# Local attention: the output product and its residual sum for two tiles at once, in every second slot

## The reference

```python
h = shift_token(x); q, k, v = split(h @ wqkv)      # 128 -> 3 x 512
q, k = l2norm(q) * qs, l2norm(k) * ksc
q, k = rotary_xpos(q, k)
o = local_attention(q, k, v)                       # own and previous window, masked
x = x + o @ wo                                     # 512 -> 128: product and residual sum
h = layer_norm(shift_token(x)); a, g = split(h @ w1 + b1)
x = x + (a * gelu(g)) @ w2 + b2
```

## Time and profile before

| | us |
|---|---|
| median of 3 runs | 2858.48 (2858.22 to 2858.83) |
| the profiled execution | 2855.07 |
| its span | 2853.3 |
| PE busy | 2602.7 (91%) |
| DVE busy | 2146.8 (75%) |
| ACT busy | 1946.6 (68%) |
| POOL busy | 1093.9 (38%) |

### The profile page before, as it was taken

One profiled execution on the slowest core, in us unless ns is written; L12 is line 12 of the kernel. 1 busy time (PEld: TensorE's weight loads), 2 busy tenths in 40 slices (PEclk: granted clock), 3 DMA queues, 4 the chain that ended last, 5 costly groups with the idle time before them and its releaser, 6 DMA issues. The chain is left out here.

```text
span 2853.3 us, 61208 instructions
## 1 busy us (share of the span) xinstructions
PE 2602.7 (91%) x21644; PEld 1731.2 (61%) x21644; DVE 2146.8 (75%) x3842; ACT 1946.6 (68%) x5521; POOL 1093.9 (38%) x1248
## 2 busy tenths in 40 slices
PE   6699898987989899888799999998989999999898
PEld 3476896764654444435557777776435777777643
DVE  4577565776766689667689999996448999999676
ACT  4477565776754544263289999997438999999744
POOL 0243343430005633210055555553215555555331
PEclk9799998998999999899899999999999999999999
DMA  4200120000000000130000000000000000000000
GB/s 149 78 24 25 52 76 24 24 24 7 9 17 1 1 0 1 32 61 1 28 2 2 2 2 2 2 2 21 1 9 2 2 2 2 2 2 2 2 26 34
DMA packets 83166, 53.87 MB, mean 19 GB/s; under 512 B 28848, under 2 KB 75568, under 8 KB 82864
## 3 DMA queue, kind: packets, MB, share of 16 engines
q1 hardware_dynamic: 78768, 41.56, 5.2%
q0 software_dynamic: 4096, 8.40, 1.0%
HBM read 31.59 MB, written 18.35 MB: 18 GB/s over the span
## 5 line engine op out<-in xcount | busy, mean ns | idle before, releaser
L2214 ACT ACTIVATE probs<-banks,minus_max,rnorm 128x128 f32<-128x128 f32 x1024 | 460.1, 469 | 4.3 <-DVE minus_max L2310 4.3
L2130 POOL TENSOR_TENSOR qk_cross<-qk_raw,rope_scaled 128x512 f32<-128x512 f32 x256 | 326.2, 1275 | 21.7 <-ACT qk_raw L2247 9.2
L2087 PE MATMUL banks<-weights,hf 128*128 128x512 f32 x512 | 276.8, 623 | 5.0 <-ACT kt L2243 5.0
L2140 POOL TENSOR_TENSOR qk_rot<-qk_rot,rnorm 128x512 f32<-128x512 f32 x128 | 133.5, 1043 | 284.6 <-DVE qk_rot L2343 284.1
L2214 ACT ACTIVATION_READ_ACCUMULATOR probs<-banks,minus_max,rnorm 128x1 f32 x1024 | 223.3, 218 | 0.0
L2290 DVE COPY probs_t<-banks 128x512 f32<-128x512 f32 x256 | 175.6, 686 | 46.0 <-PE banks L2053 46.0
L2053 PEld LDWEIGHTS banks<-ident,probs 128*128 128x128 f32 x1024 | 127.1, 141 | 136.7 <-issue 133.7
L731 ACT ACTIVATE probs<-banks,minus_max 128x128 f32<-128x128 f32 (+1 forms) x512 | 206.6, 437 | 4.9 <-DVE minus_max L759 4.7
L2336 DVE TENSOR_TENSOR qk_rot<-qk_raw,rope_scaled 128x512 f32<-128x512 f32 x256 | 175.0, 723 | 0.0
L2324 DVE TENSOR_REDUCE sumsq<-qk_sq 128x16 f32<-128x1024 f32 x128 | 154.7, 1208 | 23.0 <-issue 17.6
L2096 PE MATMUL banks<-ident,qk_rot 128*128 128x128 f32 x1024 | 159.1, 278 | 14.0 <-DVE qk_rot L2343 8.7
(11 more groups left out here) (357 smaller groups left out, 6903.7 us busy)
## 6 DMA issues: line engine op xcount, KB each, us to landing
sorted_x<-zero_rows SPq DMA_DIRECT2D x10, 512.0 KB, 6.0
rows_in<-sorted_x SPq DMA_DIRECT2D x18, 256.0 KB, 3.1
sorted_y<-rows_out SPq DMA_DIRECT2D x18, 256.0 KB, 2.4
x_res<-in_x SPq DMA_DIRECT2D x8, 512.0 KB, 6.6
out_x<-x_res SPq DMA_DIRECT2D x16, 256.0 KB, 2.0
w1b<-in_L_ffn_w SPq DMA_DIRECT2D x8, 256.0 KB, 4.1
s_branch<-in_L_ffn_w SPq DMA_DIRECT2D x8, 256.0 KB, 6.0
w1g<-in_L_ffn_W SPq DMA_DIRECT2D x8, 256.0 KB, 3.0
```

What stands on the lines that cost most here:

```text
L2087: pe.matmul(ps[:, misc(k, j)], hf[:, n // 2 % 2, 0, n % 2 * P:(n % 2 + 1) * P], wqkv[:, w:w + QW], start=True, stop=True).then_inc(*S[name ...
L2130: return pool.tensor_tensor(by_half(tw[:, n, at]), by_half(qk[:, n, at])[:, :, ::-1, :], tab[:, n, 2 * w + 1].rearrange("p (a d) -> p a d" ...
L2214: last = act.activation(pr[:, k % 2, head], ps[:, 2 * (k % 2) + par, c * P:(c + 1) * P], ACT.Exp, scale=rn[:, k % 4, head:head + 1], bias= ...
```

## The change

The output product and the residual sum are done in even slots only (`k % 2 == 0`), for tiles k-4 and k-3 together: 256 columns in place of 128. `ot` gets two halves, ScalarE's copy writes half `k % 2`. The steps o_ps and added count 2 a round in place of 4. In odd slots the k projection, which shares the bank, waits for the transposes of the slot before; in even slots, as before, for the sum.

```diff
-        o, ot = buf("attended_tok", P, QW), buf("ot", P, 4, P)
+        o, ot = buf("attended_tok", P, QW), buf("ot", P, 4, 2, P)
...
-                if here(i, k + ahead):
+                if here(i, k + ahead) and name != "added":
                     pe.wait_ge(*S[name].at(i, k + ahead))
+                    return
+                if here(i, k + ahead) and (k + ahead) % 2:
+                    pe.wait_ge(*S["added"].at(i, (k + ahead) // 2))
                     return
                 u -= 2
...
-        per.update(copied=2, v_mixed=2, exps=8, turned=8, turned_sb=8, mixed=8)
+        per.update(o_ps=2, added=2, copied=2, v_mixed=2, exps=8, turned=8, turned_sb=8, mixed=8)
...
-                    if here(i, k - 3):
+                    if k % 2 == 0 and here(i, k - 3):
                         pe_free(pe, i, k, OUT_AT)
                         for c in range(4):
-                            mm = pe.matmul(ps[:, misc(k, OUT_AT), 0:P], wo[:, c], ot[:, c], start=(c == 0), stop=(c == 3))
+                            mm = pe.matmul(ps[:, misc(k, OUT_AT), 0:T], wo[:, c], ot[:, c].rearrange("p n t -> p (n t)"),
+                                           start=(c == 0), stop=(c == 3))
                         mm.then_inc(*S["o_ps"].inc)
...
-                        act.wait_ge(*S["o_ps"].at(i, k - 3))
-                        act.activation(ot[:], bank(ps, misc(k, OT_AT), 4, P), ACT.Copy).then_inc(*S["ot_sb"].inc)
+                        act.wait_ge(*S["o_ps"].at(i, (k - 2) // 2 - 1))
+                        act.activation(ot[:, :, k % 2], bank(ps, misc(k, OT_AT), 4, P), ACT.Copy).then_inc(*S["ot_sb"].inc)
...
-                    if here(i, k - 3):
-                        xn = m["xn"][:, bass.ds((i * 4 + k - 3) * P, P)]
-                        dve.wait_ge(*S["o_ps"].at(i, k - 3))
+                    if k % 2 == 0 and here(i, k - 3):
+                        xn = m["xn"][:, bass.ds((i * 4 + k - 4) * P, T)]
+                        dve.wait_ge(*S["o_ps"].at(i, (k - 3) // 2))
                         dve.wait_ge(S["first"].sem, PRIME)
-                        dve.tensor_tensor(xn, xn, ps[:, misc(k, OUT_AT), 0:P], ALU.add).then_inc(*S["added"].inc)
+                        dve.tensor_tensor(xn, xn, ps[:, misc(k, OUT_AT), 0:T], ALU.add).then_inc(*S["added"].inc)
```

More of the change, by code:

```diff
@@ L2100, in local_attention @@
                              "rnorm", "crossed", "rotated", "unit", "qt_ps", "kt_ps", "qt_sb", "kt_sb", "scores",
-                             "rawmax", "rowmax", "rowsum", "attended", "ot_ps", "ot_sb", "o_ps", "added"], 4)
-        per.update(copied=2, v_mixed=2, exps=8, turned=8, turned_sb=8, mixed=8)
+                             "rawmax", "rowmax", "rowsum", "attended", "ot_ps", "ot_sb"], 4)
+        per.update(o_ps=2, added=2, copied=2, v_mixed=2, exps=8, turned=8, turned_sb=8, mixed=8)
         with Stage(R, **per), Stage(1, **ffn.per), nc.Block() as block:
@@ L2106, in _ @@
                 fetch(sp, ahead)
-                sp.wait_ge(*S["o_ps"].at(R - 1, 3))
+                sp.wait_ge(*S["o_ps"].at(R - 1, 1))
                 for to, at in after:
@@ L2413, in pool_program @@
                 pool.wait_ge(*S["deviation"].at(0, n - 2))
-                pool.wait_ge(*S["added"].at(n, 3))
+                pool.wait_ge(*S["added"].at(n, 1))
                 pool.tensor_copy(hs[0:64, n % 3], seqs[0:64])
@@ L2433, in pe_program @@
                 pe.wait_ge(*S["ot_sb"].at(LR - 1, 3))
-                pe.wait_ge(*S["added"].at(LR - 1, 3))
+                pe.wait_ge(*S["added"].at(LR - 1, 1))
             if f == 0 and c + 3 < R:
```

## The result

The changed kernel takes 2881.65 us (2881.42 to 2883.59, 3 runs) against 2858.48: 1.0085 times the time before, with a 95% interval of 1.0065 to 1.0105. It is slower, as forecast, by 23 us where 33 were forecast. The span of the profiled execution grew from 2853.3 to 2879.9, by 26.6 us.

A forecast was written before the change was run, and what follows sets the result against it. TensorE, ScalarE and VectorE, all nearly full, were taken to bound the kernel through tight handovers in each pair of slots. 56 pairs at +0.54 us (30.2) plus 2.6 for the tail, on 2858.5, gave 2891 us; range 2869 to 2908.

The forecast's parts named there:

- The output product: TensorE, even slots: eight matmuls of 256 columns take 1.90 us against 1.06 for 128 columns, 0.84 more.
- The residual sum and the waits on buffers: VectorE's sum falls from 0.56 to 0.42 us a pair, but is hidden; buffer waits are off the path: 0.
- The lateness in even slots passes to the odd slot in full: Even q projection to odd qt transposes: everything comes 0.84 us late, and the stretch stays 7.00 us.
- ScalarE's room in odd slots: ScalarE's wait for q, 0.21 us, is the only room before kt, so v comes 0.63 us late.
- What the odd slot's saved 0.89 turns into: TensorE, odd slots: the 0.89 us saved by having no product becomes idle time in front of v.
- The qt transposes without a wait for rotated: Start of even slots: VectorE is ahead, so TensorE's qt transposes no longer wait for it; 0.09 us gained a pair.
- The count of pairs and the tail: Local attention: 56 pairs at +0.54 us make 30.2; the last product of both layers adds 2.6 us.
- nothing is given back: Odd slots: ScalarE's 0.21 us is not regained, so a pair grows by 0.84; 2908 us, chance 0.12.
- slots average out: Odd slots' savings cover even slots' 0.84 us, TensorE being the only bound; 2858 us, no change, chance 0.06.
- weight loads set the product's time: Output product: halved loads make a wide group as short as a narrow one, 0.89 us; 2842 us, chance 0.06.
- rival 1: Odd slots: `attended` before the q projection takes the place of ScalarE's 0.21 us; +0.84 a pair, 2908 us, chance 0.12.
- Rival 4: Even slots: VectorE's run has room the rows don't show, so a pair grows only 0.25 us; 2875 us, chance 0.16.

The follow-up runs named there:

- the moved q half: VectorE's q half of the rotation's straight part put ahead of its first copy of probs; alone, on the kernel before the change: 2921.73 us.
- the fastest version: Changed kernel, with VectorE's q half of the straight rotation before its first copy of probs and ScalarE's kt after one exp, not two: 2842.70 us, 0.9955.

## Why the prediction was right, and where its sizes were off

- *The output product*: right. Eight wide matmuls take 1.89 us (1.90 forecast) and put q off by 0.87 (0.84 forecast; they also start 0.04 later after the transposes). The same-shape row of another stage was a good price.
- *The residual sum and the waits on buffers*: right, worth nothing. The run with half of the chunks in each slot shows a longer sum hidden.
- *The lateness in even slots passes to the odd slot in full*: right, 7.00 us before and after.
- *ScalarE's room in odd slots*: right in its mechanism (the two runs with shorter squares), too small in its size. The forecast took 0.21, the idle time of the row. The start of q after that of the squares fell from 1.26 to 0.94: 0.32 us. Without a wait q starts 0.11 us before the row of the squares ends (2415.74 + 1.05 = 2416.79, q at 2416.68); the idle time is counted from that end, so it understates the room. This is the mis-sized term: 0.11 a pair, 6 us over 56 pairs.
- *What the odd slot's saved 0.89 turns into*: partly wrong. The forecast had all of it, less the room, as idle time in front of v. The rows have, to a hundredth, 0.32 given back, 0.29 and 0.10 lost where q waits for `attended` and loads its weights in the open, and 0.19 more than before in front of v. It made no difference to the sum, since kt is last behind both. But two signs came out smaller than forecast: TensorE waits 0.31 for kt and not 0.6, and its busy share fell to 98.66% and not to 96, also because the modelled end of a PE row covers part of a wait (the qt transposes' row ends at 2415.20, q starts at 2415.32).
- *The qt transposes without a wait for rotated*: 0.09 forecast, 0.09 measured.
- *The count of pairs and the tail*: 56 times 0.46 makes 26 us. The tail (from the start of the last product to the next stage's matmul) grew from 2.16 to 3.45 and from 1.86 to 3.58 us, 3.0 in all against 2.6 forecast. From a layer's first q projection to that matmul the two layers grew by 14.9 and 14.4 us, 29.3 in all, close to these two terms. The feed-forward part behind each then took 1.3 us less than before, which leaves the 26.6 of the span; why it did was not traced, and the forecast had nothing for it.
- *The total*: the forecast's 32.8 is 6 more than the profiled span's growth, mostly ScalarE's room and the feed-forward parts, and 3 more again than the medians', since those grew by 23.2 only. This last difference lies in the three runs of the kernel before that the result is compared with: their median is 2858.48, while its profiled execution took 2855.07 and its later medians of 8 to 15 runs are 2855.28 to 2855.86. The run with short squares in even slots, which left the pair as it was, took 26.4 more than the kernel before on its chip, like the span.
- *The rivals*: that nothing is given back, that slots average out, and that weight loads set the product's time are excluded by the table of stretches and by the row of 1.89 us. The wait that rival 1 names, for `attended`, did appear, but did not take up the room. Rival 4 looked for more room in VectorE's run of the even slot; that stretch stayed at 7.00, and the extra room was ScalarE's. The Trainium skill's rule (TensorE: Matmul & The Clock Gate, Back-to-back issue gap), from which the prediction estimates 1.08 us for the wide group, did not hold for these f32 matmuls: it is 1.72 from the product to q, less than 1% from 8 times the first layer's spacing of 0.217.

## What to carry to other kernels

When several engines hand over to each other in every slot of a pipeline and each is over 90% busy, joining the work of two slots in one can cost nearly its full length in that slot and return, in the other, only the smallest room on the chain behind it (here 0.87 us were added and 0.41 came back); ask what the other engines do in the slot that has become shorter. Look for that room in starts, not in idle times. And before an instruction is moved into a gap, list every wait on its new neighbours (bank, operand, the other engines' queues) and what POOL does at that moment.

## What the runs showed of the hardware

- A VectorE tensor_tensor with both operands in SBUF took 1.78 us beside POOL's tensor_tensor and 0.68 alone. The Trainium skill (SBUF — State Buffer, SBUF: two separate sides) has this: of a VectorE instruction with two SBUF inputs and a GpSimd one that reads SBUF, the one that starts first keeps the other out for the whole instruction. The rows agree: where the moved q half is long (1.78, 1.10 and 1.50 us, in three kernels), its row ends about 0.54 us after POOL's crossed part does, whenever it began. The views of waits don't show this as a wait of the instruction; it only lengthens its row. POOL lost in its turn: in the fastest version its crossed part takes 3.03 us in odd slots and 2.65 in even ones.
- A matmul group that has waited pays its first weight load in the open: 1.12 against 1.02 us for the same two matmuls of 512 columns.
